# Two key tiles of PV products at a time in a fused attention and MLP layer

## The reference

```python
h = _ln(x) * (1.0 + sc1) + sh1
x = x + g1 * _gqa_attn(h, wq, wk, wv, wo)      # 16 query heads, 4 key/value heads, head size 32
h = _ln(x) * (1.0 + sc2) + sh2
x = x + g2 * _mlp(h, w1, b1, w2, b2)           # gelu, 2048 hidden features
```

## Time and profile before

| | us |
|---|---|
| median of 3 runs | 1637.91 (1637.48 to 1639.5) |
| the profiled execution, device time | 1639.16 |
| its span, first to last instruction | 1637.4 |
| PE busy | 1519.6 (93%) |
| DVE, ACT, POOL busy | 811.8, 621.2, 573.6 |
| TensorE clock granted, mean | 0.967 of full speed |
| PV products (L1050), busy | 142.4 |
| DVE row maxima (L826), busy | 345.6 |

### The profile page before, as it was taken

The page is one execution under the profiler, slowest core; times in us unless marked ns, Lnnn a source line. Parts: engine busy times, 40 slices in busy tenths (PEclk is TensorE's granted clock), DMA queues, the critical chain, the costliest instruction groups (busy, mean ns, idle before and its releaser), DMA issues. The chain is left out here.

```text
span 1637.4 us, 21353 instructions
## 1 busy us (share of the span) xinstructions
PE 1519.6 (93%) x7013; PEld 1046.8 (64%) x7013; DVE 811.8 (50%) x1356; ACT 621.2 (38%) x1116; POOL 573.6 (35%) x222
## 2 busy tenths in 40 slices
PE   7789899898999989999877999999999999999996
PEld 4545464554655545455535888888888788888885
DVE  5377756666676666666654434242423324142412
ACT  5246555555556555555552231112111121112110
POOL 0036556566567557565561002020200202020202
PEclk9879999999999999999998999999999999999998
DMA  6221414023140412304023222020010102020100
GB/s 247 64 61 40 117 36 128 20 84 97 38 123 20 144 37 63 110 29 140 20 98 97 79 83 84 1 74 10 26 58 26 58 0 83 0 83 0 35 24 26
DMA packets 68280, 104.78 MB, mean 64 GB/s; under 512 B 10465, under 2 KB 19697, under 8 KB 68233
## 3 DMA queue, kind: packets, MB, share of 16 engines
q1 hardware_dynamic: 66192, 103.74, 20.8%
q10 hardware_dynamic: 2048, 0.53, 0.2%
HBM read 55.44 MB, written 16.81 MB: 44 GB/s over the span
## 5 line engine op out<-in xcount | busy, mean ns | idle before, releaser
L826 DVE TENSOR_REDUCE neg_max<-row_bank 128x1 f32<-128x512 f32 x512 | 345.6, 688 | 209.8 <-PE row_bank L1028 206.7
L1413 PE MATMUL acc<-w_t,hidden 128*128 128x512 f32 x1536 | 370.6, 390 | 7.7 <-DVE hidden L1330 7.7
L1403 PE MATMUL up<-h,w_t 128*128 128x512 f32 x1536 | 370.9, 391 | 0.0
L1413 PEld LDWEIGHTS acc<-w_t,hidden 128*128 128x128 f32 x1536 | 287.2, 188 | 69.8 <-DVE hidden L1330 10.7
L1403 PEld LDWEIGHTS up<-h,w_t 128*128 128x128 f32 x1536 | 287.4, 188 | 58.7
L705 ACT ACTIVATE probs<-key_bank 128x512 f32<-128x512 f32 x512 | 279.9, 594 | 109.7 <-PE key_bank L1041 101.3
L1328 DVE CAST hidden<-gelu_full 128x512 fp32r<-128x512 f32 x128 | 67.5, 527 | 443.2 <-ACT gelu_full L1274 441.6
L589 POOL TENSOR_TENSOR probs_sum<-probs_sum,probs 128x2048 f32<-128x2048 f32 x62 | 283.6, 4574 | 6.1 <-ACT probs L705 2.8
L1274 ACT ACTIVATE gelu_full<-up,bias_cols 128x512 f32<-128x512 f32 x128 | 88.3, 690 | 515.1 <-PE up L1403 515.1
L1028 PE MATMUL row_bank<-k_stack,q_stack 96*128 96x512 f32 x512 | 235.9, 463 | 23.4 <-DVE neg_max L826 15.4
L1041 PE MATMUL key_bank<-q_stack,k_stack 98*128 98x512 f32 x512 | 188.8, 439 | 44.6 <-ACT probs L705 24.0
(11 more groups left out here) (117 smaller groups left out, 1025.6 us busy)
## 6 DMA issues: line engine op xcount, KB each, us to landing
q_stack<-spare SPq DMA_DIRECT2D x384, 64.0 KB, 2.0
xa<-in_x_dram SPq DMA_DIRECT2D x8, 1024.0 KB, 9.8
resid<-in_x_dram SPq DMA_DIRECT2D x8, 1024.0 KB, 6.8
x_scratch<-resid SPq DMA_DIRECT2D x8, 1024.0 KB, 4.3
xa<-x_scratch SPq DMA_DIRECT2D x8, 1024.0 KB, 5.6
spare<-in_L_cond_w_dram SPq DMA_DIRECT2D x32, 256.0 KB, 3.0
resid<-x_scratch SPq DMA_DIRECT2D x8, 1024.0 KB, 6.8
out_dram<-y SPq DMA_DIRECT2D x8, 1024.0 KB, 4.2
```

The lines of the kernel that those rows point to most:

```text
L826: nc.vector.tensor_reduce(out=neg_max[:, g % 2, i:i + 1], in_=row_bank[(g + i) % 2][:, :], op=ALU.max, axis=AX.X, negate=True).then_inc(ro ...
L1403: last = nc.tensor.matmul(up[j % 2][:, :], w1_t[i][:, kt, j * P:j * P + P], h[k][:, kt, :], start=(kt == 0 and n == 0), stop=(kt == KD - 1 ...
L1413: last = nc.tensor.matmul(acc[tt][:, :], hidden[j % 2][i][:, tt * P:tt * P + P], w2_t[k][:, j, :], start=(j == 0 and n == 0), stop=(j == N ...
```

## The change

`values` is called in slots 0 and 2 only. Slot 2 does tiles 0 and 1 of its own group, slot 0 does tiles 2 and 3 of the group before. The wait for the transposed values of the sequence moves with it from (0,1) to (0,2). After the last sequence two tiles are done instead of one. Nothing else in the program is different: the products themselves, their banks, semaphores and counts stay.

```diff
@@ -1112,11 +1112,13 @@
                     scores(b, g, kt, 1, has_last)
                     some_rows(1)
-                    if kt > 0:
-                        if (g, kt) == (0, 1):
+                    if kt == 2:
+                        if g == 0:
                             pe.wait_ge(proj_taken["act"], u.taken("VT"))
-                        values(b, g, kt - 1, is_first=not has_last and g == 0)
-                    elif prev:
+                        values(b, g, 0, is_first=not has_last and g == 0)
+                        values(b, g, 1, is_first=not has_last and g == 0)
+                    elif kt == 0 and prev:
+                        values(*prev, TT - 2)
                         values(*prev, TT - 1)
                     some_rows(1)
                     scores(b, g, kt, 2, has_last)
@@ -1139,6 +1141,7 @@
                 def after(b):
                     u = after_units()
+                    values(b, HKV - 1, TT - 2)
                     values(b, HKV - 1, TT - 1)
```

## The result

The changed kernel takes 1709.95 us (median of 4 runs, 1709.29 to 1711.19) against 1638.7 us: a ratio of 1.0429, 95% interval 1.0404 to 1.0453. That is 71 us slower. The forecast was slower by 35, with a range up to 1695. The direction was right and the size was half.

The account below looks back on a forecast made before the run. PE was taken as nearest to a bound, though not in every slot. 4.03 us a sequence gave 28 over seven, plus 2 for the rest: 1637.9 + 30 + 5 for clock = 1673 us; forecast range 1662 to 1685, wider range 1648 to 1695.

Parts of the forecast that it names:

- sum of one sequence: Attention, all slots: costs of added PV tiles less savings where PV is taken away, 4.03 us net per sequence.
- A second tile: Slots 0 and 2: a PV tile directly behind another adds two waves, 0.90 us, against 1.17 for a whole block.
- (3,1): Group 3, slot 1: with PV gone, scores and the third row can go earlier; saves 0.78 us a sequence.
- (0,3) with (1,0): Group 0 slot 3 into group 1 slot 0: earlier second row and exps, added tile inside PE's wait; saves 0.53 us.
- The rival that the edges win: Odd slots: waits are covered after all, so saved block edges make it faster by 17 us, 1621; chance 0.08.
- bracketed waits: Waits already shown in slots (0,1), (1,3), (2,3), (3,3), cited against a gain from saved block edges; no separate size.
- The clock ... I take +5: Whole attention: change in time at the lower clock level, taken as +5 us from a range of -8 to +23.
- 7 sequences take 679.63 us, 97.09 each, against 95.87: Kernel before, seven sequences against one at full clock: the 1.2 us between are stretches at 1.2 GHz.
- From none left to three a sequence: Low-clock stretches left after the change, 1.5 us each; over 7 sequences, -8 to +23 us.
- The clock rival: Attention: two more low-clock stretches of 1.5 us in each sequence, 24 us in all, giving 1692 us; chance 0.16.
- That one follows PE's wait in (1,0): O's 12 products: their low-clock stretch, costing 1.5 us, follows PE's wait in group 1 slot 0, which nearly closes.
- three places get worse and one better: PE idles more in (0,1), (2,3), (3,3) and less in (1,0); the reason given for taking +5 us.

Follow-up runs that it names:

- filled changed kernel: The changed kernel in its own order, with unused products of constant weights put into the waits of its emptied slots; 1658.91 us, ratio 1.014.
- filled kernel before: The kernel before, order unchanged, with 15 unused products of constant weights a sequence (6, 5 and 4) in three PE waits; 1622.01 us, ratio 0.9886.
- the last run: The filled kernel before, with tile 2 of group 0 moved from its slot 3 to slot 0 of group 1 and filling adapted; 1621.67 us.

## Why the prediction was wrong

Per sequence, over sequences 1 to 6, the four distances part the change:

| us a sequence | waits as they are | waits filled | the clock's part |
|---|---|---|---|
| before | 98.84 | 95.88 | 2.96 |
| changed | 107.76 | 99.96 | 7.80 |
| difference | 8.92 | 4.08 | 4.84 |

In total the same two parts are (1658.91 - 1622.01) = 36.9 us and the remaining 34.4. The first still holds some clock, for 12.1 of the 36.9 lie ahead of the first scores of (1,0) in sequence 1 (213.45 - 201.34), where the waits give 4 a sequence. In sequence 0 the filled changed kernel has products in (0,1) only, its slots 3 stay empty, and its pair in (1,0) takes 120.34 - 117.63 = 2.71 us in place of 1.85; the filled kernel before has them in (0,1) and (2,3), and its clock doesn't fall there. So by an estimate (12.1 - 4.1) 8 of the 36.9 are clock as well, and the change cost some 29 us by its waits and some 42 by the clock. They are also about what the run of the filled changed kernel took above its expectation.

**What held.** The "sum of one sequence", 4.03, measured 4.08. That it is so close is in part luck: the added tiles cost 5.04 in place of 5.44, and what was to be saved, 1.41, came to some 0.9. A second tile adds 0.86 where 0.90 was taken. From slot to slot, in the filled kernel at full clock against the rows of before, (1,2) is 0.88 longer, (2,2) 0.84, (3,0) 0.86, (3,2) 0.85, (0,0) 0.84, (2,0) 0.40 (forecast 0.55), (0,2) 0.37, (3,1) 0.66 shorter (forecast 0.78), (0,1), (1,1), (1,3), (2,1) and (2,3) the same within 0.03 (for (1,3) the forecast was 0.10 shorter), (3,3) 0.19 shorter where nothing was forecast, (0,3) with (1,0) 0.05 shorter where 0.53 was. The rival that the edges win was wrong, and its bracketed waits told so.

**The term that failed: "The clock ... I take +5".** It measured at least 34 us, some 42 with sequence 0. Its range, -8 to +23, was too low as well. Three steps under it were wrong.
- "7 sequences take 679.63 us, 97.09 each, against 95.87": the first of these seven is sequence 0, which has no output projection of a previous sequence and takes 202.20 - 115.58 = 86.62 us. Left out, the mean is 98.84, and the clock's share of it 2.96, not 1.2. It was the wrong use of the earlier trace rows, and it made the whole effect look small.
- "From none left to three a sequence", 1.5 us each. Read in steps of 1 us over the same six sequences, the granted clock falls 10 times before and 25 times after, 1.7 and 4.2 a sequence. After the change it does so behind (0,1) and (2,3) in all six, behind (0,3) and (3,3) in five, behind (1,3) in three. At 2.96 and 7.80 us that is 1.8 and 1.9 each, more than the 1.5 of the O products that priced it, as scores, rows and the pair run slow too (3.08 in place of 1.85 for the pair alone). The clock rival, which was to reach 1692, had the right mechanism and this same price.
- "That one follows PE's wait in (1,0)": of the 10 falls before the change only four do. Five follow the wait for the maxima at the end of (2,3), one follows (0,1). So most of the present falls lay where the change closes no wait. One of the five, behind (2,3):

```profile
258.00:262.00 4.00, 3.97 (x12) 0.50 0.41 102
```


The prediction weighed "three places get worse and one better". The place that was to get better, (1,0), got worse: (0,3), emptied, lowered the clock just ahead of it in five of six sequences, and the pair ran slow.

**The term that failed in the walk: "(0,3) with (1,0) ... saves 0.53".** It saved 0.05 in the filled changed kernel, and some 0.3 in the last run, whose filling differs too. The second row did come earlier, but exp r = 2 hardly did. In the filled changed kernel, on ACT:

```profile
310.70 1.32 ACTq L698 DMA_DIRECT2D q_stack<-max_row  x2
...
312.13 1.09 ACT L705 ACTIVATE probs<-key_bank 128x512 f32<-128x512 f32 x2 [1.29 <-DVE neg_max L826]
```

The scores for that exp had started at 311.07, behind the row at 310.73, so by the ordinary distance of 0.44 it could have started at 311.51. But ACT issues the two DMAs of the maxima itself, in front of that exp, and is at it until 310.70 + 1.32 = 312.02; the exp starts at 312.13. Before, with the scores r = 2 of (0,3) first:

```profile
402.59 0.64 PE L1041 MATMUL key_bank<-q_stack,k_stack 98*128 98x512 f32 x2
...
401.69 1.17 ACTq L698 DMA_DIRECT2D q_stack<-max_row  x2
403.03 1.08 ACT L705 ACTIVATE probs<-key_bank 128x512 f32<-128x512 f32 x2 [1.20 <-PE key_bank L1041]
```

The issue ended at 401.69 + 1.17 = 402.86, and the scores with 0.44 give 403.03: both ends nearly met, and only the scores' side was read. The steps of a queue that issue DMAs have to be walked like the others. It weighs 3 to 4 us in all.

**What the runs leave open.** That idle time of PE brings the falls is shown: products of constants laid into it end them in sequences 1 to 6. Which idle time brings one isn't settled. In the changed kernel the same place is followed by a fall in one sequence and not in another, and in the kernel before there is none from 404 to 500 us. With slots 1 emptied alone there is a fall behind (0,1) in each sequence, but fewer elsewhere, so the clock in all was no worse than before (0.970). And the 12 us of sequence 0 are parted only by the estimate above.

The Trainium skill (TensorE: Matmul & The Clock Gate, Part 1) has the clock released by activity. The filled kernels agree: 15 products a sequence that compute nothing brought the mean from 200 to 800 us from 0.97 to 1.00.

## What to carry to other kernels

A block of work that seems to sit in the way can be the cover of several waits at once. Price its removal by the next wait to end, slot by slot; done so, here it came out within 0.05 us of 4 a sequence, with errors of half a us that cancelled. Then ask what the matrix engine's idle time does to the clock of what runs behind it, and read the clock's present cost from like periods only. Where waits on the matrix engine can't be closed, unneeded products laid inside them may pay: 16.7 us here.

## What the runs showed that was not expected

- Extra matmuls made two kernels faster: by 16.7 us of 1638.7, and by 51 of 1710.
- The clock fell without any long wait: in the changed kernel no single wait of PE between sequences 1 and 7 was above 2.3 us. The stretches of 4 us ahead of the falls shown have PE busy for 2.4 to 3.1 us.
- The edges of a block of column-tiled products cost 0.31 us here (1.17 for a block, 0.86 for a tile inside one), but the 64 that were saved, 20 us, are outweighed by the tiles that cover no wait any more.
